# Moving weight squares to GpSimd and respacing row sends in a fused attention and mixture-of-experts kernel

## The chip, the core and the metric

One core of a Trainium2 chip runs the whole kernel in one launch. Its engines run side by side and hand work over by semaphores: TensorE (PE; its weight loads are PEld), VectorE (DVE), ScalarE (ACT), GpSimd (POOL) and SyncE (SP, which issues DMAs). The metric is the device time of one execution in microseconds; the runs below are three executions of the same program.

## The reference, cut to what matters

The input x is 1x64x128x128, read as 64 channels of 128x128. First comes a layer norm over the last axis, a layer norm over the whole tensor with weights, and attention along rows with 4 heads of 32, gated by a sigmoid. Then 8192 tokens of 128 go through a layer norm and a top-2 mixture of 8 experts with a hidden size of 512.

```python
x = x + _L0_conv_ref(_ln_c(x), ...)          # q, k, v, gate, bias, softmax, output projection
t = _to_tokens(x)
...
gate_logits = xf @ Wg + bg                    # xf = _ln_t(t)
top_w, top_i = jax.lax.top_k(gate_logits, 2)
top_w = jax.nn.softmax(top_w, axis=-1)
...
for e in range(E):
    h = jax.nn.gelu(xf @ W1[e] + b1[e], approximate=False)
    out = out + w_dense[:, e:e + 1] * (h @ W2[e] + b2[e])
```

## The kernel before

**Attention.** 32 units of 4 rows run as a software pipeline of 35 steps (`attention_steps`, `unit`): in step s the engines work on unit s (projection, scores), s-1 (exponentials, transposes), s-2 (values) and s-3 (output projection, residual). Each engine has its own written order of work for a step. ScalarE's long part is the exponentials (L852, 16 a step). GpSimd's part is two gates (`gate`, L712) for unit s-3, then the low half of the inputs of unit s (`low_x`, L700). VectorE has places "A", "B" and "D" in a step, to which `route` attaches the work of the later stage; the residual (L1063) follows place "A".

**Routing beside attention.** As soon as rows are finished they are normalised, turned on TensorE, multiplied with the gate weights, and their two best experts are picked (`pick`). This goes in batches of 12, 12, 12 and 28 rows of 128 tokens; `plan` writes out the steps. Ranks within an expert come from a matmul with a triangular matrix, positions from the ranks (`positions`). GpSimd sends each row with an indirect DMA (`scatter_rows`, L749) into a buffer in HBM in which each expert has a region. Each row goes twice: a first choice, and after all first choices of the batch have landed, VectorE writes other metadata (`second_choice`, L1234 and L1235) and the row goes again. `scatter_plan` puts the sends into steps: up to 1, 2 or 5 behind the low half of a step, what is left in the last step. The odd steps' low half waits for all earlier sends to land.

**Expert weights.** They are loaded into `shared` early (L571), and split into a high and a low half-precision part. The power-of-two scale for that comes from the sum of squares: `weight_squares` on ScalarE, one of eight 128x1024 blocks in each of steps 12 to 19 (L878, with a running sum), then a matmul with ones in step 21 (`SCALES_STEP`). High parts are ScalarE's (L890), low parts VectorE's (`split_weights`, L1352).

**The late rows.** Seven groups of 4 rows (FIRST_LATE = 9 to 15) end after attention. VectorE normalises all of them (L1142), TensorE turns them and takes gate logits, ScalarE copies between. VectorE then picks over all 28 rows, TensorE ranks them, VectorE writes positions and metadata (L1226), and GpSimd sends 56 late rows.

**Experts.** 71 tiles of 256 tokens run as a pipeline (`tile_steps`); SP loads each tile's rows into one of 23 buffers, TensorE multiplies with high and low parts, ScalarE does Gelu and weighting, VectorE splits activations. GpSimd sends each finished tile back to HBM with two indirect DMAs (`send_rows`, L778), behind the late rows in its queue. A table says which expert and rows a tile has; that of the last 42 tiles is made by VectorE after tile steps 1, 3 and 5. At the end the two results of a token are loaded and added to the residual.

Of the kernel before, what the change touches and what calls it, by code (L numbers as in the profile page):

```python
# [25 lines left out]
P = 128  # L26
# [9 lines left out]
BIG = 3.0e38  # L36
# [33 lines left out]
def build(nc, x, ln_w, ln_b, wq, wk, wv, wb, wg_w, wg_b, wrep_w, wrep_b, Wg, bg, W1, b1, W2, b2, out):  # L70
# [28 lines left out]
    IN_BUFS = 23  # L99
# [3 lines left out]
    with ExitStack() as ctx:  # L103
# [42 lines left out]
        wsq = sb("wsq", [P, 2 * HB + 1])  # L146
        hscale = sb("hscale", [P, 4])
        inv_hscale = sb("inv_hscale", [P, 4])
        y_scale = sb("y_scale", [P, 1])
        order8 = sb("order8", [P, E])  # L150
# [28 lines left out]
        wsq_all = sb("wsq_all", [P, 2 * HB + 1])  # L179
# [11 lines left out]
        rows_in = [rows_all[:, b] for b in range(LOADS)] + [pay[0][:, 2 * b:2 * b + 2, :] for b in range(IN_BUFS - LOADS)]  # L191
        most = max(n for _, n in BATCHES)
# [130 lines left out]
        wsq_ready = sem("wsq_ready")  # L323
        b1_summing = sem("b1_summing")
# [6 lines left out]
        stats_done = sem("stats_done")  # L331
        xn_ready = sem("xn_ready")
# [27 lines left out]
        y0_in = [sem(f"y0_in{g}") for g in range(3)]  # L360
        y0_added = sem("y0_added")
        y_in = [sem(f"y_in{c}") for c in range(CH)]
# [107 lines left out]
        def scatter_plan():  # L470

            open_, second_at, at = [], {}, {}
            waiting = [[b, k, 0, rank_step[b] + 1 if k == 0 else None] for b in range(3) for k in range(2)]
            for s in range(LAST):
                at[s] = []
                quota = 1 if s in scale_at else 2 if s in pool_rows_at else 5 if s < LAST - 1 else 2 * ROUTED
                for item in waiting:
                    b, k, done, start = item
                    while start is not None and start <= s and item[2] < BATCHES[b][1] and len(at[s]) < quota:
                        at[s].append((b, k, item[2]))  # L480
                        item[2] += 1
                    if k == 0 and item[2] == BATCHES[b][1] and waiting[2 * b + 1][3] is None:
                        waiting[2 * b + 1][3] = min(s + 2, LAST - 1)
                        second_at.setdefault(waiting[2 * b + 1][3], []).append(b)
            rest = [(b, k, i) for b, k, done, _ in waiting for i in range(done, BATCHES[b][1])]
            return at, second_at, rest

        scatters_at, second_at, scatters_left = scatter_plan()
        assert sorted(b for bs in second_at.values() for b in bs) == [0, 1, 2]

        def meta_count(b, k):

            order = sorted([(rank_step[c] + 1, 0, c) for c in range(3)] + [(s, 1, c) for s in second_at for c in second_at[s]])
            return order.index(next(o for o in order if o[1] == k and o[2] == b)) + 1
# [147 lines left out]
        def _(pool):  # L642
# [79 lines left out]

            def scale_rows(b, start, stop):
# [28 lines left out]
            def step(s, p):  # L752
                unit(s, p, 3, gate, 0)
                unit(s, p, 3, gate, 1)
                if p == 1 and s < UNITS:
                    for b in range(3):
                        for k in range(2):
                            wait(pool, scattered[b][k], 16 * sum((b, k) == at[:2] for t in range(s) for at in scatters_at[t]))
# [32 lines left out]
        def _(act):  # L791
# [74 lines left out]

            def gate_exponential(b):
# [3 lines left out]

            def weight_squares(j):

                n, b = divmod(j, HB)
                if j == 0:
                    act.wait_ge(ffn_in, 2 * HB * 16)
                    act.wait_ge(xs_ready, 12)
                last = nc.scalar.activation(x1[:, 0:E, :].rearrange("p r w -> p (r w)"),  # L878
                                            w_raw[n].rearrange("p r w -> p (r w)")[:, b * E * P:(b + 1) * E * P], ACT.Square,
                                            accum_out=wsq[:, j:j + 1])  # L880
                if j == 2 * HB - 1:
                    last.then_inc(wsq_ready, 1)
                else:
                    chain.link(last)
# [9 lines left out]
            def step(s, p):  # L894
# [21 lines left out]
                if 0 <= s - SQUARES_STEP < 2 * HB:  # L916
                    weight_squares(s - SQUARES_STEP)
                for j in W_HIGH_AT.get(s, ()):
                    high_weights(j)

            attention_steps(step)

            for g in LATE_GROUPS:
                copy_turned(g, late_banks[(g - FIRST_LATE) % len(late_banks)], late_xnT[g % len(late_xnT)])
            act.wait_ge(xn_ready, GROUPS)
            act.wait_ge(lg_full, GROUPS)
            nc.scalar.activation(pay[2][:, :, 0:W], pay[1][:, :, 0:W], ACT.Copy).then_inc(copied, 1)
            gate_exponential(3)

# [37 lines left out]
        def _(dve):  # L967
# [97 lines left out]
            def route(s, place):  # L1065
# [22 lines left out]
                for n, at in enumerate(((UNITS + 1, "A"), (UNITS + 1, "B"), (UNITS + 1, "D"), (UNITS + 2, "A"), (UNITS + 2, "A"))):  # L1088
# [9 lines left out]
            def step(s, p):  # L1098
# [7 lines left out]
                route(s, "A")  # L1106
                for b in second_at.get(s, ()):
                    second_choice(b)
                unit(s, p, 3, residual)
# [28 lines left out]

            def normal_rows(g, to):
# [16 lines left out]
            def take_late_logits(bank):  # L1156

                dve.wait_ge(lg_full, GROUPS)
                nc.vector.tensor_tensor(lg[:, 0:LATE, :], bank[:, 0:LATE * E].rearrange("p (i e) -> p i e", e=E),
                                        over(bgate_all[:], LATE), ALU.add).then_inc(lg_ready, len(LATE_GROUPS))  # L1160

            def pick(b, pieces=(0, 1, 2, 3)):

                first, n = BATCHES[b]
                dve.wait_ge(lg_ready, (first + n) // R)
                l, a, c, k = lg[:, 0:n, :], r_a[:, 0:n, :], r_b[:, 0:n, :], key[:, 0:n]
                for piece in pieces:
                    j, part = divmod(piece, 2)
                    t = top[j][:, 0:n]
# [6 lines left out]
                    chain.link(nc.vector.tensor_tensor(oh[j][:, 0:n, :], c, spread(k, n), ALU.is_equal))  # L1176
                    if j == 0:
                        chain.link(nc.vector.scalar_tensor_tensor(l, oh[0][:, 0:n, :], -BIG, l, ALU.mult, ALU.add))
                        continue
                    chain.link(nc.vector.memset(oh_sum[:, n:n + 1, :], 0.0))  # L1180
                    nc.vector.tensor_tensor(oh_sum[:, 0:n, :], oh[0][:, 0:n, :], oh[1][:, 0:n, :], ALU.add).then_inc(picks_ready, 1)
                    nc.vector.tensor_tensor(k, top[1][:, 0:n], top[0][:, 0:n], ALU.subtract).then_inc(gap_ready, 1)
# [92 lines left out]
            def rest_table_counts():  # L1275

                q, number, start = lists[0], lists[1], lists[2]
                low, high = slice(0, E), slice(E, LISTS)
                dve.wait_ge(ranks_read, 4)
                chain.link(nc.vector.tensor_tensor(counts[:, high], carry[4][:], region_base[:], ALU.subtract))  # L1280
                nc.vector.tensor_copy(count_at[:], counts[0:1, high]).then_inc(counts_ready, 1)
# [427 lines left out]
```

## Time and profile before

| what | value |
|---|---|
| runs | 798.38, 798.19, 798.07 us, median 798.19 |
| profiled execution | 798.93 us, span in the profile 797.1 us |
| busy share | PE 81%, DVE 78%, ACT 75%, POOL 52% |
| chain that ended last, by engine | PE 51%, DVE 26%, ACT 10%, issue 6%, POOL 3%, DMA 3% |
| granted TensorE clock, mean over the span | 0.923 of full speed |

The span is cut into stages by time: attention until about 488 us, late rows until about 514, experts until about 780, then loads, additions and stores. A share over the whole span says little, because the stages have different limits; the rows below are cut by stage.

### The profile page before, as it was taken

The page shows a single profiled execution, that of the slowest core. Times are in us where ns is not written, and L with a number is a line of the kernel's source. Part 1 is how long each engine was busy: PE and PEld are TensorE (multiplying, and loading weights), DVE is VectorE, ACT ScalarE, POOL GpSimd, SP SyncE. Part 2 cuts the span into 40 slices and gives each one's busy share as a digit, 9 for nine tenths or more (in the row PEclk, how much of TensorE's full clock was granted, in tenths as well). Part 3 has the DMA queues.
Part 4 walks back from the last instruction along what each step waited for, and adds up shares of the span by engine and source line. Part 5 has one row for each costly group of instructions (what it writes and reads, how often), then busy time and mean ns, then how long its engine had stood idle before and what let it go on. Part 6 is the DMA issues. An engine that isn't in the chain of part 4 may idle for free.

```text
span 797.1 us, 21526 instructions
## 1 busy us (share of the span) xinstructions
PE 643.7 (81%) x6886; PEld 536.6 (67%) x6886; DVE 617.8 (78%) x2322; ACT 599.2 (75%) x1518; POOL 416.1 (52%) x532
## 2 busy tenths in 40 slices
PE   0099889888998788879888858498999999999930
PEld 0098777767776676767775647376888888888720
DVE  4982678788778778977787888778888888888944
ACT  3672899999988998877886853276888888888720
POOL 7010122464245656445626544477777777777770
PEclk9999999999989999997998975589999999999985
DMA  9969100000000000001000000363123333371447
GB/s 219 270 175 211 34 3 2 2 1 2 2 2 2 8 25 5 9 21 32 32 2 31 26 28 21 87 163 92 53 67 107 99 106 99 104 256 59 167 126 280
DMA packets 55429, 60.36 MB, mean 76 GB/s; under 512 B 16502, under 2 KB 46776, under 8 KB 53786
## 3 DMA queue, kind: packets, MB, share of 16 engines
q1 hardware_dynamic: 44106, 31.97, 15.9%
q0 software_dynamic: 8704, 17.85, 6.7%
q10 hardware_dynamic: 2512, 9.18, 4.1%
q8 instruction: 60, 0.98, 0.5%
q14 instruction: 47, 0.39, 0.2%
HBM read 34.94 MB, written 24.02 MB: 74 GB/s over the span
## 4 chain that ended last, share of the span: by engine, by line
PE 51%; DVE 26%; ACT 10%; issue 6%; POOL 3%; DMA 3%; SPq 1%; ACTq 0%; POOLq 0%; DVEq 0%
PE PT L1679 10%; PE PT L1504 5%; ACT L L852 5%; PE S L1492 4%; PE B L1447 3%; PE S L1659 3%; PE S L1661 3%; PE S L1660 3%; DVE xt L1063 3%; PE B L1534 3%; POOL expert_out L778 2%; DVE L L1041 2%; DVE pl L1028 2%; PE PT L1671 2%; DVE hl L1398 2%
## 5 line engine op out<-in xcount | busy, mean ns | idle before, releaser
L749 POOL DMA_INDIRECT routed<-pay,pos x128 | 127.1, 993 | 70.3 <-issue 34.2
L947 ACT ACTIVATE hf<-S,b_sb,inv_hscale 128x256 f32<-128x256 f32 x284 | 137.4, 564 | 32.7 <-PE S L1661 31.9
L852 ACT ACTIVATE L<-L,lmin 128x128 f32<-128x128 f32 x512 | 160.4, 392 | 0.6
L1041 DVE CUSTOM_DVE_ANT_0 L<-S,biasN 128x128 f32<-128x128 f32 x512 | 117.2, 285 | 18.1 <-issue 16.7
L1398 DVE SCALAR_TENSOR_TENSOR hl<-hf,hscale,hh 128x512 f16<-128x512 f32 x142 | 106.8, 752 | 5.1
L778 POOL DMA_INDIRECT expert_out<-pay x90 | 95.3, 1058 | 27.4 <-issue 25.3
L712 POOL TENSOR_TENSOR og<-on,rden 128x256 f32<-128x256 f32 x64 | 39.5, 619 | 125.1 <-DVE on L1054 100.3
L847 ACT ACTIVATE ph<-PT 128x512 f16<-128x512 f32 x128 | 75.9, 595 | 30.8 <-PE B L1521 20.4
L700 POOL TENSOR_TENSOR xs<-x,xs 64x512 fp32r<-64x512 f32 x32 | 41.9, 1309 | 105.1 <-ACT xs L828 75.6
L1504 PE MATMUL PT<-identity,L 128*128 128x128 f32 x512 | 81.7, 297 | 16.9 <-ACT L L852 16.9
L1396 DVE TENSOR_SCALAR hh<-hf,hscale 128x512 f16<-128x512 f32 x142 | 68.8, 485 | 31.1 <-ACT hf L947 31.0
L1028 DVE TENSOR_TENSOR pl<-PT,ph 128x512 f16<-128x512 f32 x128 | 84.6, 685 | 4.6 <-ACT ph L847 4.2
L1659 PE MATMUL S<-fx_h,w_h 128*128 128x256 f16 x284 | 79.2, 279 | 8.7 <-DVE fx_l L1390 8.3
L1679 PE MATMUL PT<-w_h,hh 128*128 x568 | 78.8, 220 | 4.1 <-DVE hl L1398 3.8
L1492 PE MATMUL S<-qk_all 32*128 32x128 f32 x1024 | 79.7, 297 | 0.7 <-ACT qk_all L834 0.7
L1660 PE MATMUL S<-fx_l,w_h 128*128 128x256 f16 x284 | 79.2, 279 | 0.0
L1661 PE MATMUL S<-fx_h,w_l 128*128 128x256 f16 x284 | 79.2, 279 | 0.0
L1504 PEld LDWEIGHTS PT<-identity,L 128*128 128x128 f32 x512 | 62.6, 151 | 24.2 <-ACT L L852 19.6
L1679 PE MATMUL PT<-w_h,hl 128*128 x568 | 78.1, 219 | 0.0
L1679 PE MATMUL PT<-w_l,hh 128*128 x568 | 78.1, 219 | 0.0
L1519 PEld LDWEIGHTS B<-vh,ph 128*128 128x128 f16 x512 | 42.3, 97 | 45.4 <-issue 33.0
L1519 PE MATMUL B<-vh,ph 128*128 128x33 f16 x512 | 53.2, 181 | 24.0 <-DVE xt L1063 18.3
(284 smaller groups left out, 1746.8 us busy)
## 6 DMA issues: line engine op xcount, KB each, us to landing
pay<-routed SPq DMA_DIRECT2D x45, 130.0 KB, 2.3
shared<-expert_out SPq DMA_DIRECT2D x6, 768.0 KB, 5.5
shared<-in_L_ffn_W SPq DMA_DIRECT2D x8, 512.0 KB, 7.3
rows_all<-routed SPq DMA_DIRECT2D x26, 130.0 KB, 2.2
out<-xt SPq DMA_DIRECT2D x6, 384.0 KB
xt<-in_x SPq DMA_DIRECT2D x4, 512.0 KB, 13.1
xt<-in_x ACTq DMA_DIRECT2D x4, 512.0 KB, 9.3
routed<-pay,pos POOLq DMA_INDIRECT x128, 2.3
```

The lines of the kernel that those rows point to most:

```text
L749: pool.indirect_dma_start(routed, bass.IndirectOffsetOnAxis(ap=pos[k][:, row:row + 1], axis=0), source[:, part_row(b, i), :], None).then_i ...
L778: pool.indirect_dma_start(expert_out, bass.IndirectOffsetOnAxis(ap=row_place[t % IN_BUFS][:, k, W + 1:W + 2], axis=0), rows_in[t % IN_BUFS ...
L852: last = nc.scalar.activation(L[p][:, h, i, :], L[p][:, h, i, :], ACT.Exp, scale=-1.0, bias=lmin[p][:, h * R + i:h * R + i + 1])
L947: last = nc.scalar.activation(hf[p][:, b, :], S[2 * p + pair][:, k * TILE:(k + 1) * TILE], ACT.Gelu, scale=inv_hscale[:, 0:1], bias=b1_fla ...
L1041: last = nc.vector.tensor_tensor_reduce(out=L[p][:, h, i, :], in0=S[h][:, i * P:(i + 1) * P], in1=biasN[:, h, :], scale=-float(D) ** -0.5, ...
L1398: nc.vector.scalar_tensor_tensor(hl[p][:, b, :], hf[p][:, b, :], hscale[:, 2:3], hh[p][:, b, :], ALU.mult, ALU.subtract).then_inc(hl_ready, 1)
L1492: last = nc.tensor.matmul(S[h][:, c], q[d, c], k[d, c], start=True, stop=True)
L1504: last = nc.tensor.transpose(PT[i % 2][:, h * P:(h + 1) * P], L[p][:, h, i, :], identity[:])
L1659: nc.tensor.matmul(dst, w1_h[:, block_at], fx_h[p][:], start=True, stop=False)
L1660: nc.tensor.matmul(dst, w1_h[:, block_at], fx_l[p][:], start=False, stop=False)
L1661: last = nc.tensor.matmul(dst, w1_l[:, block_at], fx_h[p][:], start=False, stop=True)
L1679: last = nc.tensor.matmul(PT[p][:, k * P:(k + 1) * P], h_part[p][:, b, k * P:(k + 1) * P], w_part[:, block_at], start=False, stop=b == HB ...
```

## The change

- ScalarE's eight squares go to GpSimd, in steps 1 to 7: a multiplication for each of eight blocks and an addition onto a running block for six of them. VectorE sums the two blocks over columns in steps 10 and 12 (place "A"). The buffers are columns of `pay0` that rows fill from step 16 on.
- `scatter_plan` may put one send between the two gates of an even step; a batch that starts in a step gets at most two sends in it; the second choice may start one step after the last first choice instead of two. `second_choice` stands ahead of `route(s, "A")`. Worked out, the sends behind the low half of steps 17 to 34 are, before: 2 2 5 1 1 1 5 5 5 5 4 0 5 5 5 5 4 12; after: 2 2 5 1 1 5 5 5 5 0 2 5 5 5 5 2 5 5, and one more between the gates of steps 18, 20, 22, 24, 26, 28 and 30. Second choices' metadata moves from steps 24, 29, 34 to steps 21, 27, 32.
- Late groups 12, 13 and 15 are normalised by ScalarE (`scalar_rows`), two of them at the end of step 34 and one behind the copies of the first five groups; the high part of the second bias is ScalarE's in step 33.
- The picks of the last 28 rows come in two parts, 20 and 8 rows; TensorE turns the last two groups after the logits of the first five, with their logits in another bank.
- Weight splits 5 to 7 and the second positions come behind the first tile's tokens; the rest table is made in 17 parts, one behind each of tile steps 1 to 17; a Gelu on one column is issued ahead of the tiles; 24 row buffers instead of 23.

```diff
-        SQUARES_STEP, SCALES_STEP = 12, 21
+        SQUARES_AT = {1: (0,), 2: (1, 2), 3: (3,), 4: (4,), 5: (5,), 6: (6,), 7: (7,)}
+        LATE_LOGITS = 8
+        SCALAR_ROWS = (FIRST_LATE + 3, FIRST_LATE + 4, GROUPS - 1)
...
+                def take(into, new, count):
+                    for item in waiting:
+                        b, k, done, start = item
+                        while (start is not None and (start == s if new else start < s)
+                               and item[2] < BATCHES[b][1] and len(into) < count):
+                            into.append((b, k, item[2]))
+                            item[2] += 1
+                if s % 2 == 0 and s < UNITS:
+                    take(between[s], False, 1)
+                take(at[s], False, quota)
+                take(at[s], True, min(quota, len(at[s]) + 2) if s < LAST - 1 else quota)
...
-                        waiting[2 * b + 1][3] = min(s + 2, LAST - 1)
+                        waiting[2 * b + 1][3] = min(s + 1, LAST - 1)
...
+            def weight_squares(j):
+                n, b = divmod(j, HB)
+                if j == 0:
+                    pool.wait_ge(ffn_in, 2 * HB * 16)
+                raw = w_raw[n].rearrange("p r w -> p (r w)")[:, b * E * P:(b + 1) * E * P]
+                if b == 0:
+                    chain.link(nc.gpsimd.tensor_tensor(square_sum[n], raw, raw, ALU.mult))
+                    return
+                chain.link(nc.gpsimd.tensor_tensor(square_one, raw, raw, ALU.mult))
+                last = nc.gpsimd.tensor_tensor(square_sum[n], square_sum[n], square_one, ALU.add)
...
                 unit(s, p, 3, gate, 0)
+                for b, k, i in between_at[s]:
+                    scatter_rows(b, k, i)
                 unit(s, p, 3, gate, 1)
...
                 unit(s, p, 0, low_x)
+                if s in SQUARES_AT:
+                    pool.wait_ge(xs_ready, s + 1)
+                    for j in SQUARES_AT[s]:
+                        weight_squares(j)
...
+            def scalar_rows(g):
+                act.wait_ge(late_scaled, 1 if g * R < LATE_SCALES[0][1] else 2)
+                for i in range(g * R, (g + 1) * R):
+                    last = nc.scalar.activation(pay[1][:, i - ROUTED, 0:W], xt[:, i, :], ACT.Identity,
+                                                scale=rstd[:, i:i + 1], bias=shift[:, i:i + 1])
...
+                if s == UNITS + 1:
+                    second_bias_high()
+                if s == UNITS + 2:
+                    scalar_rows(SCALAR_ROWS[0])
+                    scalar_rows(SCALAR_ROWS[1])
...
+                for n, at in enumerate(((10, "A"), (12, "A"))):
+                    if (s, place) == at:
+                        dve.wait_ge(squares_made, n + 1)
+                        nc.vector.tensor_reduce(wsq[:, n:n + 1], square_sum[n], AX_X, ALU.add).then_inc(wsq_ready, 1)
...
+            early = LATE - 2 * R
+            take_late_logits(A, 0, 0, early)
+            pick(3, start=0, stop=early)
+            take_late_logits(B, LATE_LOGITS * R * E, early, LATE)
+            pick(3, start=early)
             split_weights(3)
-            take_late_logits(A)
-            pick(3)
             split_weights(4)
-            split_weights(5)
             take_ranks(3, B, 0)
             positions(3, (0, 1))
-            positions(3, (2,))
-            split_weights(6)
-            split_weights(7)
+            def behind_first_tokens():
+                positions(3, (2,))
+                for j in range(5, 2 * HB):
+                    split_weights(j)
...
-            after = {1: rest_table_counts, 3: lambda: held.extend(rest_table()), 5: lambda: rest_table_rows(*held)}
+            after = {1 + part: lambda part=part: rest_table(part) for part in range(17)}
+            after[-1] = behind_first_tokens
```

## Rows read from the trace of the kernel before

**Rows 1.** Timeline of GpSimd, first late send and last expert send (start, length).
```profile
514.08 0.96 POOL L749 DMA_INDIRECT routed<-pay,pos  x1 [9.94 <-DVE pay L1226]
...
776.70 0.96 POOL L778 DMA_INDIRECT expert_out<-rows_all  x1 [0.30 <-issue]
```
**Rows 2.** Waits of GpSimd from 514 to 797: total us, times, longest.
```profile
POOL expert_out L778 <- issue: 39.6, 130, 0.3
```
**Rows 3.** Windows cut at residuals: us, busy of PE, PEld, DVE, ACT, POOL; clock.
```profile
103.04:189.55 86.51, 77.28 (x929) 61.72 (x928) 70.50 (x376) 81.25 (x225) 34.29 (x64) 1.00 0.01 2
200.94:304.06 103.12, 90.01 (x1004) 74.20 (x1003) 78.16 (x410) 94.00 (x247) 50.08 (x84) 0.93 0.03 8
304.06:340.31 36.25, 30.78 (x373) 24.74 (x371) 34.01 (x176) 31.60 (x87) 17.07 (x39) 1.00 0.03 8
340.31:356.02 15.71, 11.66 (x121) 9.61 (x120) 11.35 (x59) 10.99 (x30) 7.39 (x8) 0.89 0.07 23
356.02:369.94 13.92, 11.97 (x128) 10.19 (x128) 11.02 (x60) 10.78 (x29) 9.96 (x11) 0.88 0.11 35
369.94:383.84 13.90, 13.44 (x129) 11.79 (x128) 8.91 (x48) 10.98 (x30) 7.64 (x9) 0.75 0.08 25
...
408.01:421.25 13.24, 11.52 (x131) 9.72 (x129) 11.38 (x61) 11.83 (x31) 2.50 (x3) 0.87 0.01 2
421.25:437.28 16.03, 12.26 (x117) 9.69 (x116) 10.41 (x60) 10.54 (x30) 11.24 (x13) 0.82 0.11 34
437.28:472.76 35.48, 26.74 (x300) 20.27 (x299) 29.90 (x145) 26.95 (x69) 19.64 (x22) 0.89 0.09 30
```
**Rows 4.** Waits of TensorE from 200.94 to 304.06, the steps with squares.
```profile
PE PT L1504 <- ACT L L852: 6.9, 7, 1.5
```
**Rows 5.** Waits of TensorE from 103.04 to 189.55, plain steps.
```profile
PE PT L1504 <- ACT L L852: 3.4, 8, 0.4
```
**Rows 6.** Groups by line and form: busy us, mean ns, idle before.
```profile
L878 ACT ACTIVATE x<-shared 128x1024 f32<-128x1024 f32 x8 | 8.4, 1046 | 0.0
L738 POOL TENSOR_TENSOR tmp_a<-tmp_a,rstd 128x8 f32<-128x8 f32 x6 | 1.3, 210 | 0.5
L712 POOL TENSOR_TENSOR og<-on,rden 128x256 f32<-128x256 f32 x64 | 39.5, 619 | 125.1 <-DVE on L1054 100.3 <-DVE rden L1053 23.9
L700 POOL TENSOR_TENSOR xs<-x,xs 64x512 fp32r<-64x512 f32 x32 | 41.9, 1309 | 105.1 <-ACT xs L828 75.6 <-ACT xs L807 29.5
L804 ACT ACTIVATE x<-xt,shift,rstd 128x128 f32<-128x128 f32 x64 | 24.9, 479 | 6.8 <-DVE shift L983 6.8
L1172 DVE TENSOR_TENSOR r_a<-lg,top 128x96 f32<-128x96 f32 x6 | 2.8, 467 | 0.2
L1173 DVE TENSOR_TENSOR r_b<-r_a,order 128x96 f32<-128x96 f32 x6 | 1.5, 258 | 0.2
L1315 DVE TENSOR_REDUCE tile_expert<-tile_both 1x42 f32<-1x672 f32 x1 | 0.8, 841 | 0.0
```
**Rows 7.** Timeline of GpSimd, step 3: two gates and low half.
```profile
94.83 0.62 POOL L712 TENSOR_TENSOR og<-on,rden 128x256 f32<-128x256 f32 x1 [4.55 <-DVE on L1054]
97.49 0.61 POOL L712 TENSOR_TENSOR og<-on,rden 128x256 f32<-128x256 f32 x1 [2.04 <-DVE on L1054]
99.31 1.27 POOL L700 TENSOR_TENSOR xs<-x,xs 64x512 fp32r<-64x512 f32 x1 [1.21 <-ACT xs L828]
```
**Rows 8.** The expert weights' loads: issue ns, first and last issue.
```profile
L571 SPq DMA_DIRECT2D shared<-in_L_ffn_W x8: 418/1725/2116, 57.3 to 66.5; - x8
```
**Rows 9.** Timeline of GpSimd: first send of step 23, gates of step 24.
```profile
341.19 1.01 POOL L749 DMA_INDIRECT routed<-pay,pos  x1 [3.99 <-DVE pay L1219]
...
347.40 1.19 POOL L712 TENSOR_TENSOR og<-on,rden 128x256 f32<-128x256 f32 x2
```
**Rows 10.** Timeline of TensorE: turn of late group 14, late ranks.
```profile
494.76 1.11 PE L1540 MATMUL S<-identity,pay 128*128 128x128 f32 x4 [1.56 <-DVE pay L1142]
...
507.41 0.35 PE L1560 MATMUL B<-oh_sum,before_h 128*128 128x232 f16 x1 [5.86 <-DVE oh_sum L1181]
```

More of the change, by code:

```diff
@@ L191, in build @@
         rows_in = [rows_all[:, b] for b in range(LOADS)] + [pay[0][:, 2 * b:2 * b + 2, :] for b in range(IN_BUFS - LOADS)]
+        free = pay[0][:].rearrange("p r w -> p (r w)")[:, 12 * ROW:]
+        square_sum = [free[:, n * E * P:(n + 1) * E * P] for n in range(2)]
+        square_one = free[:, 2 * E * P:3 * E * P]
         most = max(n for _, n in BATCHES)
@@ L1154, in take_logits, with take_late_logits, pick @@
                                         over(bgate_all[:], R), ALU.add).then_inc(lg_ready, 1)
[L1156 to L1166, printed above, removed]
+            def take_late_logits(bank, column, first, stop):
+                dve.wait_ge(lg_full, (ROUTED + stop) // R)
+                n = stop - first
+                nc.vector.tensor_tensor(lg[:, first:stop, :], bank[:, column:column + n * E].rearrange("p (i e) -> p i e", e=E),
+                                        over(bgate_all[:], n), ALU.add).then_inc(lg_ready, n // R)
+            def pick(b, pieces=(0, 1, 2, 3), start=0, stop=None):
+                first, whole = BATCHES[b]
+                stop = whole if stop is None else stop
+                n = stop - start
+                mine = slice(start, stop)
+                dve.wait_ge(lg_ready, (first + stop) // R)
+                l, a, c, k = lg[:, mine, :], r_a[:, mine, :], r_b[:, mine, :], key[:, mine]
                 for piece in pieces:
                     j, part = divmod(piece, 2)
-                    t = top[j][:, 0:n]
+                    t = top[j][:, mine]
                     if part == 0:
@@ new lines, in rest_table @@
+                if part == 8:
+                    chain.link(nc.vector.tensor_tensor(other[:, 0:LISTS], cum[:, 0:LISTS], number[:, 0:LISTS], ALU.subtract))
+                    chain.link(nc.vector.tensor_tensor(other[:, 0:LISTS], start[:, 0:LISTS], other[:, 0:LISTS], ALU.subtract))
+                if part == 9:
+                    chain.link(nc.vector.tensor_scalar(other[:, LISTS:LISTS + 1], cum[:, LISTS - 1:LISTS], -1.0,
+                                                       float(E * REGION // TILE), ALU.mult, ALU.add))
+                    chain.link(nc.vector.tensor_tensor(change[:, 0:LISTS], other[:, 1:LISTS + 1], other[:, 0:LISTS], ALU.subtract))
@@ new lines, in rest_table @@
+                if part == 13:
+                    chain.link(nc.vector.tensor_tensor(tile_cmp[:], tile_cmp[:], change[:, 0:LISTS].unsqueeze(1).broadcast_to(wide), ALU.mult))
+                if part == 14:
+                    chain.link(nc.vector.tensor_reduce(tile_row[:], tile_cmp[:], AX_X, ALU.add))
+                if part == 15:
+                    chain.link(nc.vector.scalar_tensor_tensor(tile_row[:], tile_no[:], other[:, 0:1], tile_row[:], ALU.add, ALU.add))
+                    chain.link(nc.vector.tensor_scalar(row_at[:, mine], tile_row[:], float(TILE), None, ALU.mult))
```

224 lines of the change are left out of this document (122 added, 102 removed).

## The prediction

> **What bounds the kernel now.** I read the profile from its end. The GpSimd (POOL) timeline first: from the first late row send at 514.08 to the last expert send at 776.70 GpSimd issues 198 indirect DMAs (56 sends of late rows, 142 of expert outputs) [rows 1], and the view of waits shows nothing but the issue gap of 0.3 us before the expert sends [rows 2]. That is 263.6 us for 198, 1.33 us each, without one real stall. So behind 514 us the expert stage is GpSimd's queue: TensorE could run the tiles sooner and the end would not move. Whatever gains must bring the start of that queue, 514.08, forward; that start is released by VectorE's metadata of the late rows (L1226).
>
> Before that lies attention. The windows are cut at the residual additions (L1063), one per step. Steps with attention alone take 86.51 / 8 = 10.81 us with ScalarE busy 81.25 of 86.51 [rows 3]. The eight that hold a square take 103.12 / 8 = 12.89 us, ScalarE busy 94.00 of 103.12, the granted clock 0.93 of full speed instead of 1.00. Then come three at 12.08 each, a stretch with the slow ones (15.71, 13.92, 13.90, 13.24, 16.03), and three at 11.83 before the last step. The waits say what ends last: in the square steps TensorE waits for the exponentials L852 6.9 us in 7 waits, in the plain ones 3.4 us in 8 [rows 4, 5]. ScalarE runs the square (L878) right between exponentials, so its time is on the path.
>
> **Part 1: the squares leave ScalarE.** Eight activations of 1.046 us [rows 6] leave steps 12 to 19: 8 x 1.046 = 8.4 us. Bounds: the growth of TensorE's wait alone, about 3.9 us, and 11 us if the eight steps came down to 11.5 us with the clock back at 1.00. I take 8.4, because ScalarE has the least idle time there.
>
> **Part 2: GpSimd squares in steps 1 to 7.** Eight multiplies and six additions of 128x1024 f32. The trace has none so wide. Lower bound: the slope from 0.210 us at 128x8 to 0.619 us at 128x256 [rows 6] is 1.65 ns a column, so 1.9 us; upper: the 64x512 subtraction at 1.309 us is 2.56 ns a column, so 2.6 us. The gate L712 is nearest in partitions and type; scaled whole it gives 2.48, by its slope 1.9; I take 2.3. Where do they sit? Behind the low half L700 of each step, ahead of the next step's gates. In plain steps GpSimd idles 4.55 us before the first gate and 2.04 before the second [rows 7], so steps 1 (one), 4 (one), 3, 5, 6 and 7 (two each, 4.7 us) are covered. Step 2 has four in a row: L700 ended 4.55 us before the gate at 94.83, at 90.28; 4 x 2.3 plus 0.3 of hand-overs ends at 99.8, the two gates end at 101.1 instead of 98.10, and the next L700 starts then instead of at 99.31. TensorE needs both and stands about 2.0 us: +2.0 (0.5 at 1.9 us each, 3.3 at 2.6). Queued behind the squares is the low half of step 3, late by the same amount, so it is not counted again. The weights must have landed: their last transfer is issued at 66.5 [rows 8], 24 us ahead of step 2's squares, so I charge nothing; step 1 has only one square, and a landing that is late even for step 2 would cost its lateness once.
>
> At this place a rule speaks against the move. The trace shows that VectorE operations with two SBUF inputs suffer beside GpSimd: r_a of 128x96 takes 467 ns where r_b of the same shape takes 258 [rows 6]. The Trainium skill, SBUF — State Buffer, "Who interferes with whom", says that a VectorE instruction with two SBUF inputs and a GpSimd instruction that reads SBUF exclude each other for the whole instruction; the rows agree in kind. In steps 1 to 7 VectorE's code has no such pair: logits, low halves, residuals and gates' inputs read PSUM on one side. The skill's GPSIMD Engine Reference, "Elementwise — side-by-side cycle accounting", gives about 2.6 cycles an element at 1.2 GHz; my estimate from it is 2.2 us an operation, by which step 2 would cost 1.6 instead of 2.0.
>
> The two sums over columns that VectorE now makes in steps 10 and 12 are reduces of 1024 columns; L1315 takes 0.841 for 672, so 1.25 each. VectorE is busy 70.50 of 86.51 us in the plain steps, so 2.0 us of each are free, though not all in that place: +0.6 for both (0 to 2.5).
>
> **Part 3: the sends.** In step 23 GpSimd waits 3.99 us for the metadata of the batch that starts in that very step, then issues five sends, and both gates of step 24 run back to back at 347.40 [rows 9], while a plain step has 2.04 us between them: the first was at least 2 us late. Step 29 into 30 repeats it. These are the steps of 15.71 and 16.03 us. Recomputing the plan from the diff: step 23 gets five sends of batch 0's second choice, whose metadata is written in step 21; step 29 four old sends and one new. So no step waits for metadata and then sends five. Steps 22, 24, 28 and 30 get six, but the sixth sits between the two gates, where 2.04 us are idle [rows 7]. The six other routing steps on either side average (36.25 + 35.48) / 6 = 11.96 us [rows 3]. The two worst come down to 12.0: -7.7. The three others of the five (13.92, 13.90, 13.24) lie 5.2 over; each shows a granted clock of 0.75 to 0.88, so part of it is TensorE's own: I take half, -2.5. Sum -10.2; bounds -4 (two gates, 2 us each) and -12.9. Of the second choices' sends only five instead of twelve are left in step 34, and their metadata is written two steps sooner; so they end sooner, but GpSimd then waits for late metadata all the same (9.94 us before 514.08 now [rows 1]): nothing gained there. VectorE's new place for the second choice waits for sends of the step before; these land while GpSimd's gates and low half run, so I charge nothing, and up to 2 us in each of three steps if not.
>
> **Part 4: the late rows.** ScalarE takes two groups ahead of its copies, 8 x 0.389 (24.9 us for 64 rows, L804) [rows 6] = 3.1 us, and the second bias, of which I estimate that 0.4 us reach past its idle time: the turned groups are copied 3.5 us later. TensorE had stood 1.56 us before group 14 [rows 10], so the last logits come about 1.9 us later. Against it: behind the last logits TensorE waits 5.86 us for the picks of 28 rows [rows 10]; with the first 20 picked ahead, 13 instructions on 64 columns remain, at most 13 x 0.258 = 3.4: -2.5. Net -0.5; bounds +1.9 (the split saves nothing) and -2.5 (ScalarE's part hidden).
>
> **Part 5: the rest at nothing.** The rest table in 17 parts, later weight splits, the earlier Gelu table and the 24th buffer all speed TensorE's tiles, which are covered by GpSimd's queue of 263.6 us; without that cover they would be worth some 7 us: three splits of 1024 columns at 1.25 us, by L1315's row, and four table operations of 0.84. SP loads the late tiles only once all late sends have landed, as before.
>
> **The sum.** -8.4 + 2.0 + 0.6 - 10.2 - 0.5 = -16.5. The profiled execution took 798.93, so 782.4; it lies 0.74 over the median of the runs, so 781.7 as a median.
>
> **Rivals.**
> A: the sends' plan gives little. For it: ten steps still carry five or more sends, and VectorE is busy 11.02 of 13.92 us in one of the five [rows 3]. Against it: the 3.99 us wait is in the rows. With the sends at -2 the sum is -8.3: 790.
> B: more comes. With fewer stalls TensorE keeps its full clock (0.75 to 0.93 granted in the routing steps): squares -11, sends -12.9, late -2.5, with +0.5 and +0.6: -25.3, which is 773 at the outside; 775 as its own value.
> C: slower. The squares on GpSimd cost 4.3 us or more each, through the exclusion named above. Step 2 would then stand 10 us, and four steps with two each, which have 4.55 + 2.04 us, 2.2 us each: 19 us in all, which eats the 18.5 us that the other parts give. At 5 us it is 806. Against it: all GpSimd rows of that kind run at 2.4 to 2.6 ns a column.
> D: the expert stage is not GpSimd's queue, and faster tiles come on top with the 7 us of part 5: 775. Against it: the queue's waits.
> E: the change does not reach the end, because late metadata waits for something fixed. Nothing of the kind is in the chain: about no change.
>
> **How the numbers follow.** Forecast 0.61, A 0.17, B 0.10, C 0.06, D 0.04, E 0.02. The likeliest gives 781.7. The range takes in A and most of B and leaves out C, E and the edge of B: 773.5 to 790. Within 0.2% (1.6 us), about what runs of this kernel can tell from no change, lies E alone: 0.02; slower is C with a little more for waits that I missed, 0.07; faster 0.91.
>
> **What would show it.** Steps 12 to 19 near 11.8 us with TensorE's wait for L852 back at 0.4 us; GpSimd operations of 1.9 to 2.6 us and one gap of some 2 us in step 2 or 3; no step over 14 us between 340 and 440; GpSimd's late sends starting 16 us sooner and running 263 us without a wait. The prediction is wrong if the squares take over 4 us, if GpSimd idles behind that start, or if the steps of 12.9 us stay where they are although ScalarE is relieved.

## Result and the profile after

The changed kernel takes 791.28 us (median of four runs, 789.77 to 791.40) where the kernel before took 798.19: the ratio is 0.991, with an interval of 0.989 to 0.993. It is faster, by about 7 us; the forecast was 781.7 with a range that ends at 773.5 and 790.0. The profiled execution took 791.40, span 789.2, against 798.93 and 797.1. One execution of the kernel before (825.81 us) and one with the old sends (1019.63 us) were slow ones, and no median here counts them.

Windows of the profile after, cut at the residuals (now L1121) as in the kernel before (the clock stands third from the end of a line): the eight plain steps, the eight that held a square, three, the five long ones of [rows 3] (first, second, third, then two), and three.

```profile
120.61:208.05 87.44, 77.98 (x934) 62.14 (x932) 72.77 (x378) 82.15 (x228) 51.04 (x74) 1.00 0.01 2
208.05:305.89 97.84, 88.94 (x1004) 73.93 (x1003) 77.41 (x410) 85.24 (x231) 51.73 (x86) 0.93 0.03 9
305.89:342.14 36.25, 30.77 (x373) 24.75 (x371) 33.99 (x177) 31.76 (x88) 24.45 (x47) 1.00 0.06 19
342.14:354.55 12.41, 10.01 (x121) 8.19 (x120) 11.24 (x58) 10.58 (x29) 9.18 (x11) 1.00 0.12 39
354.55:368.24 13.69, 12.26 (x129) 10.21 (x128) 11.02 (x60) 11.18 (x30) 7.17 (x8) 0.88 0.08 27
368.24:380.62 12.38, 11.92 (x129) 10.12 (x128) 9.02 (x49) 10.38 (x29) 5.54 (x7) 0.86 0.07 23
405.08:417.47 12.39, 10.44 (x131) 8.08 (x129) 11.01 (x59) 11.53 (x30) 6.71 (x8) 1.00 0.08 23
417.47:428.78 11.31, 9.71 (x117) 7.75 (x116) 10.56 (x61) 10.40 (x31) 8.56 (x10) 1.00 0.12 38
428.78:464.87 36.09, 26.40 (x298) 20.78 (x298) 30.31 (x149) 26.83 (x70) 18.92 (x22) 0.86 0.09 29
```

The five long steps fell from 72.80 us to 62.18, none of them over 14 now; the square steps from 103.12 to 97.84, with 8.8 us of ScalarE's busy time gone from them. TensorE's wait for the exponentials in the square steps (total, times, longest), 6.9 us in [rows 4], is:

```profile
PE PT L1590 <- ACT L L897: 0.4, 2, 0.2
PE A L1564 <- DVE vl L1080: 2.8, 3, 1.3
```

The second line is a wait for VectorE that was 0.4 us at its counterpart before; it took part of the place. (The first window is cut one residual later than its counterpart; cut alike, at 109.94 and 196.52, it is 86.58 against 86.51.)

What was lost stands ahead of the first line. GpSimd's timeline in step 2:

```profile
90.34 1.27 POOL L722 TENSOR_TENSOR xs<-x,xs 64x512 fp32r<-64x512 f32 x1 [9.32 <-ACT xs L873]
91.69 1.89 POOL L754 TENSOR_TENSOR pay<-shared 128x1024 f32<-128x1024 f32 x1
93.66 2.38 POOL L755 TENSOR_TENSOR pay<-pay 128x1024 f32<-128x1024 f32 x1
96.12 1.90 POOL L754 TENSOR_TENSOR pay<-shared 128x1024 f32<-128x1024 f32 x1
98.09 2.35 POOL L755 TENSOR_TENSOR pay<-pay 128x1024 f32<-128x1024 f32 x1
100.52 1.19 POOL L734 TENSOR_TENSOR og<-on,rden 128x256 f32<-128x256 f32 x2
```

The four operations take 8.5 us, and both gates follow back to back from 100.52, where [rows 7] had them at 94.83 and 97.49. TensorE feels it through two other engines: ScalarE's next activations (L885, L886) wait for the first gate, VectorE waits for the second of them, and TensorE for VectorE. Then the windows of that wait and behind it; in them PE's busy time follows the length:

```profile
101.23 0.38 ACT L885 ACTIVATE gt<-A 128x256 f32<-128x256 f32 x1 [2.31 <-POOL og L734]
101.92 0.43 DVE L1080 TENSOR_TENSOR vl<-A,vh 128x256 f16<-128x256 f32 x1 [2.89 <-ACT vh L886]
102.40 0.57 PE L1564 MATMUL A<-w4h,xs 128*128 128x256 f32 x1 [2.33 <-DVE vl L1080]
```

```profile
100.07:102.40 2.33, 0.00 (x0) 0.00 (x0) 0.48 (x2) 1.15 (x3) 1.56 (x3) 1.00 0.00 0
102.50:109.00 6.50, 6.50 (x32) 5.47 (x33) 3.24 (x20) 4.78 (x13) 5.52 (x3) 0.50 0.00 0
104.30:109.94 5.64, 5.64 (x27) 4.07 (x26) 1.44 (x11) 3.86 (x11) 4.33 (x3) 0.56 0.00 0
109.94:115.00 5.06, 4.22 (x75) 3.44 (x73) 4.37 (x24) 4.03 (x12) 0.62 (x1) 1.00 0.02 6
```

While TensorE stands still for 2.3 us, the granted clock is 1.00; as it starts again the clock falls to 0.50, the lower of its two levels (1.2 of 2.4 GHz), and stays there for at least 6.5 us in which TensorE is busy without a gap. From the first low half of step 1 (77.78) to the first residual (109.94) it is 32.16 us, against 26.52 before (76.52 to 103.04): 5.6 us for step 2, not 2.0. It splits at the matmul behind the wait, L1564 (L1478 before): that one comes 24.62 us behind the low half instead of 21.77 (98.29 before), so 2.8 us late, and from it to the residual it is 7.54 us instead of 4.75, 2.8 us that go with the low clock.

GpSimd's queue of sends answers to [rows 1, 2]: it starts 8.4 us sooner and again shows no wait over 0.3 us before the expert sends.

```profile
505.70 0.96 POOL L788 DMA_INDIRECT routed<-pay,pos  x1 [28.66 <-DVE pay L1304]
...
768.89 0.95 POOL L823 DMA_INDIRECT expert_out<-pay  x1 [0.30 <-issue]
```

```profile
POOL expert_out L823 <- issue: 39.6, 130, 0.3
```

The account of the two first profiles, in us, from low half to low half, residual to residual and late start to last send:

| term | forecast | measured |
|---|---|---|
| start, up to the first low half | 0 | +1.3 |
| GpSimd's squares in step 2 | +2.0 | +5.6 |
| steps 3 to 10 | 0 | +0.1 |
| squares off ScalarE, with the two column sums | -7.8 | -5.1 |
| sends | -10.2 | -9.7 |
| late rows, up to GpSimd's late start | -0.5 | -0.5 |
| GpSimd's queue of 198 sends | 0 | +0.6 |
| sum | -16.5 | -7.7 |

Three rows are off by more than a microsecond: the start, step 2 and the squares. Each was looked into by itself.

### The profile page after: what moved, and what is told of

It reads as the page before. It is cut to its first block, busy times and chain, and to the rows that moved or that the text cites. A ratio compares the mean times of both kernels' runs of the same rounds, so it can differ in the third digit from the quotient of the medians.

```text
span 789.2 us, 21562 instructions
## 1 busy us (share of the span) xinstructions
PE 636.1 (81%) x6886; PEld 531.0 (67%) x6886; DVE 619.9 (79%) x2326; ACT 597.1 (76%) x1518; POOL 445.8 (56%) x546
## 4 chain that ended last, share of the span: by engine, by line
PE 51%; DVE 25%; ACT 8%; issue 6%; POOL 6%; DMA 3%; POOLq 0%; ACTq 0%; SPq 0%; DVEq 0%
PE PT L1777 10%; PE PT L1590 5%; POOL expert_out L823 5%; PE S L1578 4%; ACT L L897 4%; PE B L1533 3%; DVE L L1099 3%; DVE pl L1086 3%; DVE xt L1121 3%; PE S L1757 3%; PE S L1759 3%; PE S L1758 3%; PE B L1620 2%; DVE rowstat L525 2%; PE A L1638 2%
## 5 line engine op out<-in xcount | busy, mean ns | idle before, releaser
L823 POOL DMA_INDIRECT expert_out<-pay x94 | 97.7, 1040 | 28.6 <-issue 26.5
```

What stands on the lines that cost most here:

```text
L823: pool.indirect_dma_start(expert_out, bass.IndirectOffsetOnAxis(ap=row_place[t % IN_BUFS][:, k, W + 1:W + 2], axis=0), rows_in[t % IN_BUFS ...
```

## Experiments

**Step 2's squares moved.** Theory: the whole 5.6 us come from the four GpSimd operations ahead of the next gates, partly as a stall and for the rest as the clock behind it.

```diff
-SQUARES_AT = {1: (0,), 2: (1, 2), 3: (3,), 4: (4,), 5: (5,), 6: (6,), 7: (7,)}
+SQUARES_AT = {1: (0, 1, 2), 2: (3,), 3: (4,), 4: (5,), 5: (6,), 6: (7,)}
```

> The same squares, but the four GpSimd operations of step 2 move: step 1 makes three squares (five operations, about 10.6 us at the 1.89 and 2.37 us read after the change, in the 9.3 us or more that GpSimd idles there), steps 2 to 6 one each. Theory: TensorE's stall of 2.3 us in step 2 and the half granted clock behind it (0.56 in the window 104.30 to 109.94) come from these four operations alone. Then the first residual comes at 104.3 instead of 109.94, the clock stands at 1.00 there, and the time is 785.7. Rival 1, stall alone: the clock falls there anyway, -2.3 us, 789.0. Rival 2: the late first residual is loading and start-up, or the wider GpSimd work slows its neighbours wherever it runs; then nothing moves, 791.3.

Measured: 783.74 us (five runs), 0.981 of before, interval 0.978 to 0.983. The first residual comes at 104.34, as the theory had it. GpSimd's timeline (last operation of step 1's squares, low half, first gate), the matmul that waited, and the window up to that residual:

```profile
87.47 2.36 POOL L755 TENSOR_TENSOR pay<-pay 128x1024 f32<-128x1024 f32 x1
90.33 1.27 POOL L722 TENSOR_TENSOR xs<-x,xs 64x512 fp32r<-64x512 f32 x1 [0.51 <-ACT xs L873]
...
96.61 0.61 POOL L734 TENSOR_TENSOR og<-on,rden 128x256 f32<-128x256 f32 x1 [0.59 <-POOL pay L755]
```

```profile
99.59 0.39 PE L1564 MATMUL A<-w4h,xs 128*128 128x256 f32 x1
```

```profile
98.30:104.34 6.04, 5.45 (x42) 4.25 (x43) 4.10 (x23) 5.76 (x16) 3.77 (x3) 1.00 0.01 3
```

Five operations fit into the idle time of step 1, with 0.51 us to spare, the low half is not late, TensorE does not wait, and the clock stays at 1.00. From low half to residual it is 26.57 us, the last 4.75 of them behind L1564, as in the kernel before. The same work, placed 11 us sooner, costs nothing here; the 5.6 us were a matter of place alone. Against the first runs of the changed kernel the time falls 7.5 us and not 5.6: 1.4 of the rest is the window of the next experiment, and other single windows differ by -0.8 to +1.3 us. Against the kernel with the moved sums below, measured beside it, it falls 6.3.

**The column sums moved.** Steps 12 to 19 gave 5.3 us where 8.4 were forecast. One window, 208.05 to 222.38, took 14.33 us at a granted clock of 0.76, and VectorE's second sum (1.22 us) stands right ahead of it.

```diff
-for n, at in enumerate(((10, "A"), (12, "A"))):
+for n, at in enumerate(((8, "A"), (10, "A"))):
```

> VectorE's two column sums move from steps 10 and 12 to steps 8 and 10; all else as after the change. Theory: the window of 14.33 us from 208.05 to 222.38 (granted clock 0.76) comes from the second sum, 1.22 us just ahead of the residual that TensorE waits for, at a place where the first gate logits have been added to the step. Then that window comes down to about 11.7 and the time by 2.6 us, to 788.7. Rival: the window is long because of the first gate logits in it (before the change its granted clock was lowest there too); then it keeps 13 us or more and the time stays at 791.3. A third way: the sum does the same harm in step 8, and the loss only moves there.

Measured: 790.02 us, and that window is 12.89. This looks like what the theory forecasts, but it is not: in the experiments with the squares moved, with three squares in step 2 and with the old sends, which kept the sums in steps 10 and 12, the same window took 12.89, 12.92 and 12.88. The theory falls. What the second sum does cost shows one window earlier: 11.38 here, 11.53 with the sum in it, 0.15 us.

**The changed kernel again**, with no edit.

> The changed kernel once more, for the window of the first gate logits. It took 14.33 us (granted clock 0.76) in the first profile, and 12.88 to 12.92 in the four experiments so far, three of which kept the column sums in steps 10 and 12; so the theory that the second sum costs it has fallen. What is left: that 1.4 us belong to the one execution. Then the window is near 12.9 here too, and the time about 790. If 14.33 comes back, something in the changed kernel as a whole holds the clock down there, and it is 791.3.

Measured: 790.75 us (788.03 to 794.39), and the window is 12.96. The same window of the first profile, of this one, and of the experiment with the late rows (below):

```profile
208.05:222.38 14.33, 13.70 (x131) 12.14 (x130) 9.76 (x51) 11.01 (x30) 2.56 (x4) 0.76 0.01 2
207.44:220.40 12.96, 12.34 (x131) 10.92 (x130) 9.76 (x51) 11.02 (x30) 2.53 (x4) 0.87 0.01 2
208.95:220.98 12.03, 11.25 (x131) 9.33 (x130) 9.61 (x51) 10.60 (x29) 2.53 (x4) 1.00 0.01 2
```

With the same 131 matmuls its length goes with the granted clock. In the ten profiles of changed kernels it lies between 12.03 and 14.34 (14.34 with part 5 undone), and in the two of the kernel before it is 13.07 and 12.97; the 1.4 us belonged to single executions and not to the change. The eight square steps together take 96.45 here, so these steps give -6.7 against the first profile of before, and -5.6 against its second (102.09, below).

**Three squares in step 2.** If a stall of 2.3 us costs 5.6, what does one of 6.6 cost?

```diff
-SQUARES_AT = {1: (0,), 2: (1, 2), 3: (3,), 4: (4,), 5: (5,), 6: (6,), 7: (7,)}
+SQUARES_AT = {1: (0,), 2: (1, 2, 3), 3: (4,), 4: (5,), 5: (6,), 6: (7,)}
```

> Step 2 takes three squares (six GpSimd operations) instead of two (four), step 3 one and no later step more than one. The extra square is 4.26 us by the rows after the change, all of it ahead of step 2's gates, so TensorE's stall there grows from 2.3 to 6.6 us. Theory, a stall and a clock cost behind it that does not grow with the stall (3.3 us): the first residual comes 4.3 us later, at 114.2, and the time is 795.5. Rival, the clock's cost grows with the stall (5.6 us lost for 2.3 us of stall): 10.3 us later, 801.5. Second rival, that step 2 was not waiting for the squares: no change, 791.3.

Measured: 794.62 us, first residual at 115.01. TensorE's wait, and the windows from it to the residual:

```profile
106.97 0.58 PE L1564 MATMUL A<-w4h,xs 128*128 128x256 f32 x1 [6.71 <-DVE vl L1080]
```

```profile
100.00:104.30 4.30, 0.26 (x3) 0.02 (x1) 0.00 (x0) 0.00 (x0) 4.14 (x3) 0.81 0.00 2
104.30:109.30 5.00, 2.33 (x11) 2.00 (x11) 2.63 (x12) 3.04 (x8) 3.44 (x5) 0.50 0.00 0
109.30:115.01 5.71, 5.71 (x25) 4.15 (x26) 1.19 (x10) 3.62 (x10) 1.61 (x1) 0.50 0.00 0
```

From low half to residual it is 37.03 us, 10.5 over the kernel before: L1564 comes 7.2 late, and behind it stand 8.04 us instead of 4.75, 3.3 of clock. With two squares in the step, six profiles lie 4.9 to 6.1 over it: in all of them L1564 is 2.8 late, with waits of 2.3 to 3.1, and the stretch behind it takes 6.82 to 8.05, so 2.1 to 3.3 of clock. In the five profiles without the stall that stretch takes 4.74 or 4.75. A stall more than twice as long adds nothing to the clock's share; the rival in which it grows with the stall (801.5) is out.

**The old plan of sends** in the changed kernel, with the second choice behind `route(s, "A")` again.

```diff
-if s % 2 == 0 and s < UNITS:
-    take(between[s], False, 1)
-take(at[s], False, quota)
-take(at[s], True, min(quota, len(at[s]) + 2) if s < LAST - 1 else quota)
+    while start is not None and start <= s and item[2] < BATCHES[b][1] and len(at[s]) < quota:
...
-            waiting[2 * b + 1][3] = min(s + 1, LAST - 1)
+            waiting[2 * b + 1][3] = min(s + 2, LAST - 1)
```

> The new kernel with the old plan of sends: up to five a step as they come, none between the gates, the second choice written two steps after the last send of the first. Theory (the prediction's third part, read as right): the five slow steps come back to the 72.8 us that they took before, net +9.7 us, 801.0. Rival A: the sends' plan gives little, and the five steps became shorter because of something else, such as VectorE's order; then +2 us, 793.3.

Measured: 799.00 us, 1.001 of before (0.999 to 1.002), and 9.0 over the kernel with the moved sums, measured beside it; between the same residuals of these two profiles it is 9.7. Windows of the two worst steps, and GpSimd's timeline at the first:

```profile
340.87:356.58 15.71, 11.66 (x121) 9.62 (x120) 11.26 (x59) 10.99 (x30) 7.38 (x8) 0.89 0.07 22
419.88:436.37 16.49, 12.49 (x116) 10.25 (x116) 10.47 (x61) 10.44 (x29) 11.71 (x13) 0.79 0.12 38
```

```profile
341.75 1.01 POOL L777 DMA_INDIRECT routed<-pay,pos  x1 [3.98 <-DVE pay L1286]
...
347.95 1.18 POOL L723 TENSOR_TENSOR og<-on,rden 128x256 f32<-128x256 f32 x2
```

The wait for metadata, the five sends behind it and the two late gates are back as in [rows 9], and so are the 15.71 us. Without its sends the change is worth nothing in the total: what the squares give is eaten by step 2 and the start. Rival A is out.

**Part 5 undone.** The rest table, the later splits and positions and the early Gelu go back; 24 buffers stay.

```diff
-def behind_first_tokens():
-    positions(3, (2,))
-    for j in range(5, 2 * HB):
-        split_weights(j)
+positions(3, (2,))
+for j in range(5, 2 * HB):
+    split_weights(j)
...
-after = {1 + part: lambda part=part: rest_table(part) for part in range(17)}
-after[-1] = behind_first_tokens
+pieces = {1: range(0, 4), 3: range(4, 11), 5: range(11, 17)}
+after = {at: lambda parts=parts: [rest_table(part) for part in parts] for at, parts in pieces.items()}
...
-nc.scalar.activation(gtmp[:, 0:1], hscale[:, 0:1], ACT.Gelu)
```

> The changed kernel with the old last part: the last positions and the three last weight splits stand ahead of the tiles again, the rest table is made in three pieces between tiles 1, 3 and 5 instead of seventeen, and ScalarE's early load of the Gelu table is left out (24 buffers stay). Theory, the prediction's fifth part: GpSimd's queue of 198 sends runs from its start without a wait and covers all of this; the end does not move (790 to 791.3), although TensorE's first tiles come some 7 us later. Rival D: the tiles are not covered, and it costs 3 to 7 us, 794 to 798.

Measured: 790.31 us, beside 790.75 of the changed kernel in the same runs. TensorE's first product of the tiles, and the first and last sends of GpSimd's queue:

```profile
514.34 0.39 PE L1753 MATMUL S<-fx_h,w_h 128*128 128x256 f16 x1 [6.87 <-DVE fx_l L1472]
```

```profile
509.64 0.96 POOL L788 DMA_INDIRECT routed<-pay,pos  x1 [28.80 <-DVE pay L1303]
...
771.60 0.96 POOL L823 DMA_INDIRECT expert_out<-pay  x1 [0.30 <-issue]
```

The first product comes 4.7 us behind the first late send, where the changed kernel has it 0.3 us ahead (505.38 to 505.70): the tiles start 5.0 us later. GpSimd's queue takes 261.96 us from first to last all the same (263.19 in the changed kernel). Part 5 is covered, and rival D is out.

**Late rows between the copies.** TensorE waited 2.89 us for the first turned group, because ScalarE normalised two groups (8 x 0.39 us) ahead of all its copies.

```diff
-if s == UNITS + 2:
-    scalar_rows(SCALAR_ROWS[0])
-    scalar_rows(SCALAR_ROWS[1])
...
 for g in range(FIRST_LATE, GROUPS - 2):
+    if g + 1 in SCALAR_ROWS:
+        scalar_rows(g + 1)
     copy_late_turned(g)
```

> ScalarE still normalises the groups 13 and 14 of late rows (counted by the program's own numbers: the fourth and fifth late group), but between its copies of the turned groups, each one group ahead of the copy that TensorE needs last, not ahead of all copies. Theory: TensorE's wait of 2.89 us for the first copy goes, since ScalarE idles 1.85 to 2.43 us before each later copy and a group takes 1.6 us; the last logits and GpSimd's first late send come 2.3 us sooner, and the time is 788 where the changed kernel takes 790.3. Rival: another wait takes its place (TensorE waits for the rows themselves, or the last picks for the last residual), and the time stays.

(The two groups are 12 and 13 in the program's numbers; the expectation counted one too high.) Measured: 786.59 us, 4.2 under the changed kernel in the same runs. TensorE's first late logits, first in the changed kernel and then here:

```profile
479.29 1.87 PE L1638 MATMUL A<-wg_sb,L 128*128 128x8 f32 x8 [2.89 <-ACT L L910]
```

```profile
473.75 1.91 PE L1627 MATMUL PT<-identity,pay 128*128 128x128 f32 x8
475.50 1.87 PE L1637 MATMUL A<-wg_sb,L 128*128 128x8 f32 x8
```

The wait is gone, and what the place gives reaches GpSimd: from the last residual to GpSimd's late start it is 26.47 us (475.43 to 501.90) instead of 29.53, so 3.1 us are gained, 0.8 more than expected. The other 1.1 of the 4.2 lie within the spread of these runs.

**Both mends.** The diffs of the first and of the last experiment together.

> Both mends together: three squares in step 1 and one a step in steps 2 to 6, and ScalarE's late rows between its copies. If the two act at different places and add up, 783.7 - 2.3 = 781.4. Rival: the late rows wait for something fixed, and it stays at 783.7.

Measured: 780.72 us (779.14 to 783.80), 0.979 of before, interval 0.975 to 0.983: the fastest version by its median, 10 us under the changed kernel. The two add up, as far as the spread of the runs lets one see.

**The kernel before again, and GpSimd's first subtractions later.** The first low half came 1.3 to 1.5 us later in every profile of a changed kernel so far, though no part of the change acts there. In the first case there is no edit; in the second, to both mends:

```diff
 pool.wait_ge(w4_copied, 2)
+pool.wait_ge(rows_ready, 1)
 for f in range(2):
     last = nc.gpsimd.tensor_tensor(w4l[k, f], w4[k], w4h[k], ALU.subtract)
```

> The kernel before once more, for the start that no part of the prediction covers. In its first profile VectorE's row statistics begin at 7.77 and GpSimd's first low half at 76.52; in all nine profiles of changed kernels they begin at 7.8 to 8.25 and the low half at 77.8 to 78.0, because two VectorE operations with two inputs (0.17 us elsewhere) take 1.16 and 1.13 us beside GpSimd's two subtractions of 15.66 to 18.28. Theory: whether the two meet hangs on some 0.3 us in the landing of the first rows, which differs between executions; then the kernel before may show either, and a low half near 77.8 where VectorE begins late. Rival: the kernel before never meets them, and 1.3 us are a price of the change; then 76.5 again.

> Both mends, and GpSimd's two subtractions for the low part of the projection weights wait until VectorE has written the first row shifts; TensorE needs them some 30 us later. Theory: VectorE's two-input operations of 1.16 and 1.13 us go back to 0.17, the first shifts come 2 us sooner, and GpSimd's first low half comes at 76.6 to 77.2 instead of 77.99; the time falls by about 1.0 us, to 779.7. Rival: the long operations are something else that stands at that moment (a transfer, the instructions themselves); then they stay, and so does 780.7.

Measured for the kernel before: 798.67 us in one run, and the first low half at 77.79. So the unchanged kernel shows the late start too, and it is no price of the change. (In the changed kernels the statistics begin at 8.24 to 8.72, not at 7.8 to 8.25 as the expectation has it; here at 8.19.) Its VectorE and GpSimd at that moment:

```profile
15.77 1.17 DVE L66 SCALAR_TENSOR_TENSOR tmp_b<-tmp_a,rstd 128x16 f32<-128x16 f32 x1
16.97 0.17 DVE L67 SCALAR_TENSOR_TENSOR rstd<-tmp_b,rstd 128x16 f32<-128x16 f32 x1
17.18 1.12 DVE L983 SCALAR_TENSOR_TENSOR shift<-mean,rstd 128x16 f32<-128x16 f32 x1
```

```profile
15.65 2.62 POOL L688 TENSOR_TENSOR w4l<-og,w4h 64x512 fp32r<-64x512 f32 x2 [0.59 <-ACT w4h L800]
```

Both long operations have two SBUF inputs, start beside one of GpSimd's two subtractions, and end about where that one ends; with the wait of the edit they take 0.17. The last step of that chain, and GpSimd's subtractions, then read:

```profile
16.33 0.17 DVE L1041 SCALAR_TENSOR_TENSOR shift<-mean,rstd 128x16 f32<-128x16 f32 x1
```

```profile
16.68 2.60 POOL L711 TENSOR_TENSOR w4l<-og,w4h 64x512 fp32r<-64x512 f32 x2 [1.67 <-DVE shift L1041]
```

The shifts come 2.0 us sooner than with both mends alone (18.32) and the first low half at 77.04 instead of 77.99, inside the expected 76.6 to 77.2. The other half microsecond up to the 76.52 of the first profile of before does not come back. The time does not show it: 781.87 us (779.97 to 785.01), 0.978 of before, where it was 0.979 without the wait. The gain of 0.95 us is read from the trace; in the total it drowns, since in this profile the window that ends at 329.10 took 17.16 us, with a granted clock of 0.63 from 314.90 to 327.70, where eight other changed profiles have 11.8 to 12.1, and the one with part 5 undone has 16.67 at 0.59.

## Why the prediction was wrong

**What bounds the kernel** held. GpSimd's queue ran unbroken in every profile, and it hid 5 us of later tiles; each gain came through its start.

**Part 1, the squares off ScalarE**, was too large: -7.8 with the column sums was taken, and -5.1 was read in the first profile, -6.5 and -5.5 from the changed kernel's second against the two of before; all inside the stated bounds. TensorE's wait for the exponentials in these steps did fall, from 6.9 us to 0.4, as forecast. But ScalarE's whole 8.4 us were not on the path: 2.8 us of waiting for VectorE stand where 0.4 stood, and the steps take 12.06 us on average in the second profile, not 11.8. Part of the rest is the clock: the step with the first gate logits took 12.03 us at 1.00 and 12.9 to 14.3 below it, and 12.97 and 13.07 in the kernel before.

**Part 2, GpSimd's squares in step 2**, is the step that failed. Much of what it names was right: the operations (1.90 and 2.36 us, taken as 2.3, bounds 1.9 and 2.6), their place, and the late gates (they end at 101.71 against 101.1, and by the late start of 1.3 that is 0.6 sooner than forecast). The path was other than told: the next low half came at 103.10 and not right behind the gates, and TensorE stood for the gates alone, through ScalarE's and VectorE's waits for them. By the Trainium skill, GPSIMD Engine Reference, "Elementwise — side-by-side cycle accounting", the estimate was 2.2, and it lies between the two measured forms. What was left out is what a stall does to TensorE's clock (and rival C, which priced slower operations, is out by the same rows). TensorE's next matmul was 2.8 us late, where 2.0 were taken, and the stretch behind it, at a granted clock of 0.50, took another 2.8. The bounds of 0.5 to 3.3 for that step priced the operations only, so the true 4.9 to 6.1 could not lie in them. Rival B had the clock only as a gain, in the routing steps.

By the Trainium skill, "TensorE: Matmul & The Clock Gate", "Part 1: The HAM clock gate", the lower level (1.2 of 2.4 GHz) is the state in which the array rests and activity releases it, and the point of the change shifts from run to run. The window at 0.50 agrees with the level, and the stretch behind the same wait agrees with the shift (6.82 to 8.05 us in six profiles). That the same lies behind the spread of other windows was not tried.

The two column sums were sized at +0.6 and cost 0.15 for the one that was moved out of its window.

**Part 3, the sends**, was right: -10.2 forecast, -9.7 read, 9.0 in the medians and 9.7 in the profiles when undone. **Part 4** was right as a sum, -0.5; within it the late first copy (2.89 us of wait, of which about 1.9 were seen coming) was larger and could be had back by order alone. **Part 5** was right: nothing, because of the queue.

**The start**, +1.3, had no term. The prediction's baseline was one profile of before in which VectorE had finished its shifts at 15.36, just ahead of GpSimd's subtractions; the second profile of the same kernel shows 1.3 us more. VectorE's operations of 0.17 us took 1.17 and 1.12 beside the subtractions. That is the rule which the prediction named for rival C (the Trainium skill, SBUF — State Buffer, "Who interferes with whom"), that a VectorE instruction with two SBUF inputs contends with a GpSimd instruction that reads SBUF, seen at a place where it was not looked for. The squares themselves did no harm of this kind, as the prediction argued: with them, eight plain steps take 86.58 us, and 86.51 without.

Together: +3.6 for step 2 (2.8 of it the clock and 0.8 the late matmul), +2.7 for the squares, +1.3 for the start and 1.2 of small terms are the 8.8 us between -16.5 and the account's -7.7. Why the clock falls in one execution of the same step and not in another (12.03 to 14.34, 11.82 to 17.16) was not tried and stays open. It falls without such a stall, too: in the window of 14.33 TensorE's longest wait was 0.64 us.

Three smaller slips of the working change nothing: the growth of TensorE's wait is 6.9 - 3.4 = 3.5, not 3.9; 1024 columns at the rate of L1315 are 1.28 us, not 1.25; eleven steps of the new plan send five behind the low half, counting the last, not ten. And r_a's 467 ns, set against r_b's 258, is a mean of 0.68 and 0.26 us; r_b has two SBUF inputs as well, so the two forms do not tell one and two inputs apart.

## What to carry to other kernels

A stall of TensorE is not priced by its length alone: here a stall of 2.3 us cost 5.6 and one of 6.7 cost 10.5, with 2.1 to 3.3 us of low clock in each of seven profiles. When work moves to an engine that TensorE depends on, count the idle time of every single step, not the sum over them, and put the surplus into the step that has room; GpSimd had 11.2 us in step 1 (1.9 of a square and 9.32 idle) and 4.55 in step 2. And take the baseline's start from two profiles before a term of a microsecond is read into it.

## What the hardware showed

- Behind a stall of 2.3 us the granted clock was 0.50 for at least 6.5 us, with TensorE busy all the time, and 1.00 in the same step without the stall: the same stretch of work took 7.54 us instead of 4.75.
- One attention step with the same 131 matmuls took 12.03, 12.96 and 14.33 us at a granted clock of 1.00, 0.87 and 0.76, in three executions.
- GpSimd's 128x1024 operation takes 1.90 us where both inputs are the same block and 2.36 where they are two.
- A VectorE operation of 0.17 us took 1.17 beside a GpSimd operation with two SBUF inputs. In the two profiles of the kernel before, the one in which they met had its first rows 0.4 us later (8.19 against 7.77).
